# A GpSimd step reordered, and variance plus epsilon computed on VectorE

## The reference

```
x = x + xattn(ctx, layernorm(x))   # q from layernorm(x), k and v from ctx
x = x + moe(layernorm(x))
```

## Time and profile before

| what | value |
|---|---|
| median of 3 runs | 2064.0 us |
| profiled execution, its span | 2064.2 us, 2062.4 us |
| TensorE matmul busy | 1845.0 us (89%) |
| VectorE busy | 1581.6 us (77%) |
| GpSimd busy | 1469.7 us (71%) |
| ScalarE busy | 1429.1 us (69%) |
| DMA | 432.12 MB, mean 210 GB/s |

### The profile page before, as it was taken

The page is one execution under the profiler, slowest core; times in us unless marked ns, Lnnn a source line. Parts: engine busy times, 40 slices in busy tenths (PEclk is TensorE's granted clock), DMA queues, the critical chain, the costliest instruction groups (busy, mean ns, idle before and its releaser), DMA issues.

```text
span 2062.4 us, 73301 instructions
## 1 busy us (share of the span) xinstructions
PE 1845.0 (89%) x20840; PEld 1398.6 (68%) x20840; DVE 1581.6 (77%) x3919; ACT 1429.1 (69%) x3063; POOL 1469.7 (71%) x2311
## 2 busy tenths in 40 slices
PE   3899989989998999988899998899897899989997
PEld 3566666666666666666666666666664799989996
DVE  3688888888778888788788878887886677767775
ACT  2687777777777777777777777777776455545553
POOL 5467777777777777777777777777776566656665
PEclk8899999999999999999999999999998899999998
DMA  5998887788878788888788888877994788868885
GB/s 137 228 240 208 204 199 196 195 201 205 201 191 205 192 200 202 205 197 203 186 192 201 201 205 197 200 198 190 240 226 168 226 265 262 258 201 265 261 265 168
DMA packets 616925, 432.12 MB, mean 210 GB/s; under 512 B 447811, under 2 KB 562634, under 8 KB 616400
## 3 DMA queue, kind: packets, MB, share of 16 engines
q1 hardware_dynamic: 556528, 319.91, 65.1%
q0 software_dynamic: 32256, 84.47, 11.5%
q10 hardware_dynamic: 28000, 26.03, 4.2%
HBM read 234.59 MB, written 197.72 MB: 210 GB/s over the span
## 4 chain that ended last, share of the span: by engine, by line
PE 42%; POOL 22%; issue 19%; DMA 6%; DVE 6%; ACT 3%; POOLq 1%; SPq 1%; ACTq 0%; DVEq 0%
POOL rows_dram L1368 6%; PE ms_ps L774 6%; PE mx_ps L506 4%; DMA rows_dram<-rowt,posi 4%; PE o_ps L540 4%; POOL w_dn_sb L1337 4%; PE ms_ps L568 3%; PE mx_ps L568 3%; PE mx_ps L570 3%; PE mx_ps L569 3%; PE st_ps L752 3%; POOL att L1346 3%; PE o_ps L551 3%; PE ms_ps L569 3%; PE ms_ps L570 2%
## 5 line engine op out<-in xcount | busy, mean ns | idle before, releaser
L998 DVE TENSOR_REDUCE mx<-mx_ps 128x8 f32<-128x1024 f32 x512 | 625.9, 1222 | 142.6 <-PE mx_ps L506 126.8
L858 ACT ACTIVATE prob<-st_ps 128x1024 f32<-128x1024 f32 x512 | 524.0, 1023 | 156.3 <-PE st_ps L499 138.1
L506 PE MATMUL mx_ps<-stacks 48*128 48x128 bf16 x4096 | 320.4, 219 | 42.9 <-DVE mx L998 36.9
L1368 POOL DMA_INDIRECT rows_dram<-rowt,posi x256 | 259.0, 1012 | 111.8 <-POOL rowt L1362 50.8
L540 PE MATMUL o_ps<-prob,v_sb 128*32 128x256 f32 x4096 | 330.0, 394 | 0.1
L499 PE MATMUL st_ps<-stacks 50*128 50x128 bf16 x4096 | 318.6, 218 | 1.2 <-ACT prob L858 1.2
L506 PEld LDWEIGHTS mx_ps<-stacks 48*128 48x128 bf16 x4096 | 232.1, 95 | 116.8 <-issue 44.0
L568 PE MATMUL ms_ps<-e_lo 128*128 128x256 f32 x768 | 239.0, 311 | 24.0 <-ACT rank L825 14.8
L499 PEld LDWEIGHTS st_ps<-stacks 50*128 50x128 bf16 x4096 | 229.8, 94 | 2.9 <-ACT prob L858 2.0
L569 PE MATMUL ms_ps<-e_lo 128*128 128x256 f32 x768 | 220.2, 287 | 0.0
L570 PE MATMUL ms_ps<-e_lo 128*128 128x256 f32 x768 | 219.5, 286 | 0.0
(11 more groups left out here) (153 smaller groups left out, 4778.9 us busy)
## 6 DMA issues: line engine op xcount, KB each, us to landing
stack_dram<-w_dn_sb SPq DMA_DIRECT2D x768, 128.0 KB
stacks<-stack_dram SPq DMA_DIRECT2D x512, 192.0 KB
stacks<-rows_dram SPq DMA_DIRECT2D x288, 130.0 KB
w_dn_sb<-in_x SPq DMA_DIRECT2D x64, 256.0 KB, 3.1
w_dn_sb<-in_ctxT SPq DMA_DIRECT2D x64, 256.0 KB
x_res<-in_x SPq DMA_DIRECT2D x64, 256.0 KB, 2.8
stacks<-sums_dram SPq DMA_DIRECT2D x78, 128.0 KB
stacks<-base_dram SPq DMA_DIRECT2D x76, 128.0 KB
```

The source lines that it names most:

```text
L506: return pe.matmul(mx_ps[k % 2][:, i * P:(i + 1) * P], q_st[p][64 * h:64 * h + ROWS, u, j, :], k_st[p][64 * h:64 * h + ROWS, u, j, :], sta ...
L858: nc.scalar.activation(prob_all[n % 2][:, :], st_all[:, :], ACT.Exp, scale=float(HALF) ** -0.5).then_inc(a_exp, 1)
L998: v.tensor_reduce(mx[:, u, c * CHUNK:(c + 2) * CHUNK], mx_all[:, :].rearrange("p (c n) -> p c n", c=2 * CHUNK), AX.X, ALU.max).then_inc(v_ ...
L1368: g.indirect_dma_start(rows_dram[k][:, :], bass.IndirectOffsetOnAxis(ap=posi[p][:, u, k:k + 1], axis=0), rowt[p][:, u, :], None).then_inc( ...
```

## The change

GpSimd's step takes another order. `numbers` comes first. The third scatter moves from before `residual(d, 3)` to behind the two `split`s, next to the fourth. The first norm's `norm_terms` moves from before the fourth scatter to behind `split_maxima(b, 0)`. The addition of eps is taken out of `norm_terms` and done by VectorE, for the first norm in slot 1 and for the second in slot 2; `norm_terms` waits for VectorE's result in place of its own.

```
+            def with_eps(s, mv, ve_n, v_s, v_ve):
+                wait(dve, v_s, 2, s, 2)
+                v.tensor_scalar(ve_n[:, :], mv[:, :, 1], EPS, None, ALU.add).then_inc(v_ve, 1)
...
+                    if n == 1 and do_xs:
+                        with_eps(xs, mv1, ve1, v_s1, v_ve1)
                     if n == 1 and do_d:
                         combine(d, 3)
...
                     if n == 2 and do_r:
                         shared_gate(r)
                         shared_up(r)
+                    if n == 2 and do_d:
+                        with_eps(d, mv2, ve2, v_s2, v_ve2)
...
-            def norm_terms(s, mv, nb, ve_n, v_s, g_ve, g_r, g_nb):
-                wait(gp, v_s, 2, s, 2)
-                g.tensor_scalar(ve_n[:, :], mv[:, :, 1], EPS, None, ALU.add).then_inc(g_ve, 1)
-                wait(gp, g_ve, 1, s, 1)
+            def norm_terms(s, mv, nb, ve_n, v_ve, g_r, g_nb):
+                wait(gp, v_ve, 1, s, 1)
                 g.tensor_tensor(mv[:, :, 1], ve_n[:, :], neghalf[:, :], ALU.pow).then_inc(g_r, 1)
...
+                if do_r3:
+                    numbers(r3)
                 if do_k:
                     key_rest(k2)
                 if do_d:
                     residual(d, 2)
                 if do_r3:
-                    numbers(r3)
                     ready(r3)
                     scatter(r3, 0, 0)
                     scatter(r3, 0, 1)
-                    scatter(r3, 1, 0)
                 if do_d:
                     residual(d, 3)
                 if do_k:
                     split(k2, q_rest, qp, a_qb, g_qs)
                     split(k2, k_rest, kp, a_kb, g_ks)
-                if do_xs:
-                    norm_terms(xs, mv1, nb1, ve1, v_s1, g_ve1, g_r1, g_nb1)
                 if do_r3:
+                    scatter(r3, 1, 0)
                     scatter(r3, 1, 1)
                 if do_b:
                     split_maxima(b, 0)
+                if do_xs:
+                    norm_terms(xs, mv1, nb1, ve1, v_ve1, g_r1, g_nb1)
                 if do_d:
-                    norm_terms(d, mv2, nb2, ve2, v_s2, g_ve2, g_r2, g_nb2)
+                    norm_terms(d, mv2, nb2, ve2, v_ve2, g_r2, g_nb2)
```

More of the change, by code:

```diff
@@ L256, in program @@
                                                  sem("g_nb2"))
-        v_base, g_ve1, g_ve2 = sem("v_base"), sem("g_ve1"), sem("g_ve2")
+        v_base, v_ve1, v_ve2 = sem("v_base"), sem("v_ve1"), sem("v_ve2")
         passed = sem("passed")
```

## The result

The changed kernel takes 1965.5 us (median of 4 runs, 1965.1 to 1967.6) beside 2065.0 us (median of 4, 2062.7 to 2071.0) for the kernel before: a ratio of 0.9516, 95% interval 0.9494 to 0.9537. Its profiled execution took 1967.6 us. The forecast was 1956 us, 0.5% under that.

A forecast was written before the change was run, and what follows sets the result against it. The prediction took a ring through GpSimd's split and TensorE's L556 as the bound, 23.96 us a step. Falling to 22.0 over 54 steps gains 105.8 us, plus 2 elsewhere: 2064.2 - 108 = 1956 us, range 1936 to 2018.

The forecast's parts named there:

- the ring: GpSimd's split, transpose L556, TensorE slots 5 to 7, last maximum, next cast: 23.96 us a step, forecast 21.64.
- The leg from cast to cast: On GpSimd from the cast for u = 1 to that for u = 0: 14.17 us, forecast 2.32 shorter.
- 1.82: Microseconds the leg was to lose by moving the first norm's `norm_terms` behind the split: 2.12 less a 0.30 gap.
- GpSimd alone: GpSimd's own step without waits for others: 22.90 us, less 0.82 for eps and 0.50 for `numbers`, 21.58.
- the four circles: Bounds on a step after the change: L556's ring 21.64, ScalarE 21.77 to 22.08, GpSimd 21.58, TensorE 21.63 us.
- the ScalarE circle: The ring by ScalarE: L568 starts 0.44 us later against the cast, so a step is 21.77 to 22.08 us.
- What was late next: First norm's `nb`, ready 2.2 us after the cast, delays ScalarE in slot 4; L568 can start 6.0 after the cast.
- The step used as a trial: Written-out step from 1493.4 to 1515.1 us, without a first norm: 21.70 us, taken as the step forecast, but for dearer waits.
- 22.9: Step in us if ScalarE takes GpSimd's place, waiting for `nb` and late scatters: time 2007 us; chance 14%.
- the second rival: DMA engines bound the loop: stacks come late at a share of 0.85, step 23.1 us, time 2018; chance 7%.
- the slow side: Rival that VectorE's maxima in slots 2 to 4 set TensorE's pace: 0.44 us a step added, 2088 us; chance 5%.
- the other direction: Rival that each VectorE addition holds GpSimd for its length: 0.44 us a step, step 22.4, time 1978; chance 6%.

## Why the prediction was right

- *The reading of the ring was right.* The leg from cast to cast lost 2.29 us against 2.32, L556 stopped waiting, and putting the first norm back brought L556's wait back (1.12 us a step, before 1.24).
- *`numbers` first was mis-sized.* The prediction took 0.50 us, from a gap of 0.82 falling to a scatter's usual 0.30. The gap fell by 0.13 (0.84 to 0.71 in the mean), and undoing the edit cost 0.15 a step. The row nearest to a scatter behind `ready` was the one in place, not the one behind another scatter; the bound of 0, which the prediction kept, was the nearer end. The first leg lost its 2.29 all the same, 0.34 more than 1.82 and 0.13: its mean had been 0.24 above the step shown (14.41 against 14.17).
- *So GpSimd alone was mis-sized.* Forecast 21.58 us a step. It now runs through the loop with next to no wait for another engine, and its steps alternate between 21.93 and 22.22, 22.08 in the mean. Of the 0.50 too little, 0.37 is `numbers`. Another 0.29 is a gap that the prediction had taken for a wait for ScalarE and subtracted (0.47 less 0.18): it is still there at 815.18, 0.53 long, though ScalarE's operation had ended at 814.31, before the gap began. Shorter scatters (3.95 us for the four in the step shown, before 4.05) give 0.10 back, and the last 0.06 isn't accounted for. On this chip it is the highest of the four circles, where the prediction had the ScalarE circle at 21.77 to 22.08. That the wrong circle's 22.08 is also what GpSimd's measures is luck, and it kept the forecast near. Three odd steps (23.8, 23.0 and 23.6 us) bring the mean to 22.15. The forecast of 22.0 was 0.15 low, about 8 us over the loop's 52 steps. The rest was a miscount: the prediction took 54 such steps and 2 us for the others, so 5.9 us outside the loop, where 2.3 came. (By its own sum a step of 21.65 us gives 1937, not 1936, as the range's lower end.)
- *Eps on VectorE was covered,* as forecast, though its size was off both ways: 0.16 beside a scatter, 0.65 beside `split`, so 0.8 a step where 0.44 was taken (0.16 to 0.43 each were the bounds, and 0.65 is outside them). On chip C a third addition cost nothing.
- *The third scatter was right in sign.* VectorE's wait for `x` fell by 1.35 us a step, L562's by 0.45. On chip C undoing it costs 0.85 a step, by another wait than named.
- *What was late next was right.* `nb` was forecast ready 2.2 us after the cast and up to 0.9 us late for slot 4; ScalarE starts 2.12 after the cast and has waited 0.97. The key projection starts 6.15 after the cast (809.53 to 815.68), forecast 6.0.
- *The step used as a trial.* The written-out step took 21.70 us before and 20.98 after. So 21.70 was no floor; the loop came down to 0.5 us above it.

The rivals: ScalarE did wait for `nb`, but the scatters gave back all of their wait (1.16 to 0.01), so 22.9 didn't come. The DMA share rose to 0.92, more than the 0.85 of the second rival, but the stacks didn't come late: no wait for SyncE's transfers shows from 400 to 1350 us. Two of the three odd steps hold a scatter of `base_dram` that starts 1.96 us late with no releaser. On the slow side, a third addition that costs nothing excludes VectorE as the bound of slots 2 to 4 on chip C, where it has more idle time than on the first. GpSimd wasn't held: `split` took 1.16 us as before, with the additions beside half of them, and scatters of `rows_dram` 0.96 to 1.06 (before 0.96 to 1.08).

What stays open: why TensorE's results reach VectorE and ScalarE only behind a running scatter on the other chips, where the same kernels take 6 to 8% more, and at once on the first.

## What to carry to other kernels

Follow a late engine's wait round the whole loop and price each circle: a part's worth is the distance to the next circle, here four edits gained 86 to 87 us together on B and C, undoing one of them alone cost 6 to 52 us, and two of them alone gained nothing on A, where another stall stayed in. Take a gap's size behind an edit from a row that has the same instruction behind the same waits, not from the best gap of its kind. When the engine that was the culprit runs without a wait, its own instructions are the next thing to shorten or hand over, the small ones with a dependency first. A wait for another engine doesn't prove that an engine has time to spare: see whether what it waits for follows its own last instruction at a fixed distance.

## What the runs showed of the hardware

**A small VectorE operation waits for GpSimd's elementwise operation to end.** The additions of eps on the first chip, duration in ns as minimum, median, maximum:

```profile
L1033 DVE TENSOR_SCALAR ve<-mv x114: 157/442/748, 158.4 to 1431.7; 128x2 f32<-128x2 f32 x114
```

In the prediction's row of such an addition it was 216 ns. Between 400 and 1350 us, 43 of the 86 begin beside a `split` (L1344) and take 0.56 to 0.75 us; all 43 end 0.01 to 0.04 us after that `split` ends, as at 807.15 and 807.12 in the rows above. The 41 beside a scatter take 0.16 in the median. On chip C, where one of 82 begins beside a `split`, the median of 112 is 162 ns. The Trainium skill, "SBUF — State Buffer", "SBUF: two separate sides", says that of GpSimd and a VectorE operation in a two-port mode the one which starts first has the shared port pair for its whole instruction; the trace agrees, with VectorE as the one that waits. The prediction had looked for the other direction.

**A clock that falls in some kernels of a chip and not in others.** With 1.8 us of idle time ahead of slot 3, in the step shown, TensorE ran some 6 us at 0.50 behind it; with the same stall gone the loop's clock is 1.00.

**TensorE's results reach the others late beside an indirect scatter of GpSimd, on some chips.** While an indirect scatter runs, a reduction that waits for TensorE starts 0.04 us behind the matmul record on the first chip (76 cases) and 0.7 to 1.4 behind it on chip C (nine in ten of 111), 0.55 to 0.86 behind the scatter's end. With a third scatter in a row the lag in slot 2 is 2.0 to 2.3 us in the median, in three kernels on A and C.

**Chips differ.** The kernel before takes 2065, 2187, 2207 and 2209 us on four chips, and an order of work that is worth 4.8% on one is worth 3.7 to 3.9% on others.
